# End of a cross-attention stage: row norms moved into the last step, norm rows transposed first, exponentials between value copies, gate products behind

## The reference

```python
# first attention: 16 heads of width 128, 64 context rows per batch entry
q = (hidden_states @ Wq).reshape(B, Sq, H, D)
k = (encoder_hidden_states @ Wk).reshape(B, Skv, H, D)
v = (encoder_hidden_states @ Wv).reshape(B, Skv, H, D)
q = rmsnorm(q, gq)
k = rmsnorm(k, gk)
scores = jnp.einsum('bqhd,bkhd->bhqk', q, k) * scale
attn = jax.nn.softmax(scores, axis=-1)
out = jnp.einsum('bhqk,bkhd->bqhd', attn, v)
out = out.reshape(B, Sq, H * D)
return out @ Wo
...
# routing of the first mixture, on the layer norm of the updated x
logits = x.astype(jnp.float32) @ router_weight.astype(jnp.float32).T
scores = jax.nn.sigmoid(logits)
sc = scores + e_bias
...
# expert that all tokens share
return jax.nn.silu(x @ sh_gate) * (x @ sh_up) @ sh_down
...
x = x + jnp.tanh(g_xattn[0]) * _L0_xattn_ref(_layernorm(x, axis=-1), ctx_1024, ...)
x = x + jnp.tanh(g_ffn[0]) * _L0_ffn_ref(_layernorm(x, axis=-1), ...)
```

## Time and profile before

| | |
|---|---|
| median of 3 runs | 1200.52 us (1198.31 to 1205.0) |
| profiled execution | 1197.71 us, span 1196.0 us |
| PE busy | 940.9 us, 79% of the span |
| DVE busy | 717.1 us, 60% |
| ACT busy | 430.6 us, 36% |
| POOL busy | 277.6 us, 23% |
| granted TensorE clock, mean | 0.878 |

### The profile page before, as it was taken

The page is one execution under the profiler, slowest core; times in us unless marked ns, Lnnn a source line. Parts: engine busy times, 40 slices in busy tenths (PEclk is TensorE's granted clock), DMA queues, the critical chain, the costliest instruction groups (busy, mean ns, idle before and its releaser), DMA issues.

```text
span 1196.0 us, 16300 instructions
## 1 busy us (share of the span) xinstructions
PE 940.9 (79%) x5499; PEld 792.4 (66%) x5499; DVE 717.1 (60%) x1677; ACT 430.6 (36%) x809; POOL 277.6 (23%) x225
## 2 busy tenths in 40 slices
PE   4998999999977700766676746868868999999998
PEld 3877868868855500655565533544547989899898
DVE  7267677686479998222222577988976445444343
ACT  4556446565463400111111114444453233323322
POOL 0332304314200000678888710101100000000000
PEclk9998999999988655778878867998868999999899
DMA  8002200000000060688888563000000000000000
GB/s 297 4 1 71 83 1 1 1 1 1 1 1 22 22 167 0 153 176 180 182 170 174 96 189 146 1 3 1 1 1 1 1 19 1 1 18 0 18 1 18
DMA packets 58945, 66.48 MB, mean 56 GB/s; under 512 B 5069, under 2 KB 55687, under 8 KB 58119
## 3 DMA queue, kind: packets, MB, share of 16 engines
q1 hardware_dynamic: 45236, 46.45, 12.5%
q0 software_dynamic: 12288, 18.88, 8.9%
q10 hardware_dynamic: 1363, 0.37, 0.1%
HBM read 48.13 MB, written 17.56 MB: 55 GB/s over the span
## 4 chain that ended last, share of the span: by engine, by line
PE 53%; DVE 23%; issue 10%; POOL 5%; DMA 4%; ACT 4%; ACTq 0%; DVEq 0%; POOLq 0%; SPq 0%
PE bank L2062 13%; PE bank L1753 7%; PE bank L2088 7%; PE bank L1738 4%; PE bank L1710 3%; POOL acc L507 3%; DMA acc<-y,dst_now 3%; PE bank L1946 3%; PE bank L1729 2%; POOL xg L497 2%; PE bank L2073 2%; DVE cand L926 2%; DVE keyT L929 2%; DVE newton L582 1%; DVE small L1071 1%
## 5 line engine op out<-in xcount | busy, mean ns | idle before, releaser
L2062 PE MATMUL bank<-gu_hi,xnT_split 128*128 128x352 f32 x640 | 164.0, 330 | 4.9 <-DVE soft L1249 3.7
L486 POOL TENSOR_TENSOR q_lo<-soft,q_hi 128x512 fp32r<-128x512 f32 x64 | 91.3, 1426 | 226.0 <-ACT soft L1385 225.9
L2062 PEld LDWEIGHTS bank<-gu_hi,xnT_split 128*128 128x128 f32 x640 | 114.6, 192 | 5.6 <-DVE soft L1249 3.9
L507 POOL DMA_INDIRECT acc<-y,dst_now x64 | 102.5, 1602 | 26.3 <-issue 20.2
L2062 PE MATMUL bank<-gu_lo,xnT_split 128*128 128x352 f32 x320 | 104.4, 326 | 0.0
L732 DVE COPY qT<-bank 128x512 f32<-128x512 f32 x64 | 44.2, 691 | 91.7 <-PE bank L1753 91.1
L1249 DVE SCALAR_TENSOR_TENSOR soft<-sg,combine_w,bank 128x176 f32<-128x176 f32 x160 | 56.4, 395 | 70.9 <-PE bank L2062 65.3
L497 POOL DMA_INDIRECT xg<-table,src_now x64 | 64.1, 1002 | 116.6 <-DVE src_now L959 97.4
L979 DVE TENSOR_SCALAR y<-bank,xg 128x256 f32<-128x256 f32 x64 | 28.0, 479 | 95.9 <-PE bank L1874 80.2
L1598 ACT ACTIVATE sg<-bank 128x352 f32<-128x352 f32 x80 | 37.1, 465 | 127.3 <-PE bank L2062 123.3
L1861 PEld LDWEIGHTS bank<-xgT,w_gu 128*88 128x88 f32 x512 | 76.8, 196 | 7.3 <-issue 5.1
(11 more groups left out here) (271 smaller groups left out, 2209.4 us busy)
## 6 DMA issues: line engine op xcount, KB each, us to landing
w_gu<-in_L_ffn_w_gu SPq DMA_DIRECT2D x32, 352.0 KB
w_dn<-in_L_ffn_w_down SPq DMA_DIRECT2D x32, 176.0 KB
acc<-zeros SPq DMA_DIRECT2D x2, 2176.0 KB
acc_rows<-acc SPq DMA_DIRECT2D x8, 512.0 KB, 4.9
gu<-in_L_gu SPq DMA_DIRECT2D x1, 3520.0 KB, 13.4
table<-xw SPq DMA_DIRECT2D x4, 640.0 KB, 3.5
wo<-in_L_xattn_Wo SPq DMA_DIRECT2D x2, 1024.0 KB, 15.6
wq<-in_L_xattn_Wq SPq DMA_DIRECT2D x1, 2048.0 KB, 17.9
```

The costliest lines, as they stand in the source:

```text
L486: pool.tensor_tensor(q2_lo[:, h % 3, :], q2[h % 2], q2_hi[:, h % 3, :], ALU.subtract).then_inc(q2_split, 1)
L507: pool.indirect_dma_start(acc[e], bass.IndirectOffsetOnAxis(ap=dst_now[:, q, e:e + 1], axis=0), y[:, q, e, :], None, compute_op=ALU.add).t ...
L2062: mm = pe.matmul(b[:, 0:2 * F1], v[:, c, j * P:(j + 1) * P], w[:, c, p, o, :], start=(n == 0), stop=(n == len(terms) - 1))
```

## The change

VectorE: the last step now makes the row statistics and roots of group 0 behind heads 12 and 15 and applies them before it copies `n_rows`; the residual of tile 3 of group 2 goes behind Newton's steps; `normed(0)` behind the step is gone; `shared_product(0)` moves from the softmax loop into `route(0)`, behind the keys. ScalarE: the tokens and the table rows are copied first; the eight value banks are copied in three portions, one behind each of the exponentials 0, 1 and 2; then come the sigmoid, `attn_out(0)`, exponential 3, and the other `attn_out`; the silu moves behind the end of the stage. TensorE: `n_rows` is transposed before the output of tile 3 of group 2; then token transposes, that output, the logits, the values, the tiles of group 3; the gate products move behind the end of the stage.

```diff
@@ VectorE
-                    if h == 12 and not last:
-                        row_stats(i + 1)
-                    if h == 15 and not last:
+                    if h == 12:
+                        row_stats(0 if last else i + 1)
+                    if h == 15:
                         row_roots(EPS0)
-                if not last:
-                    row_apply(i + 1)
+                row_apply(0 if last else i + 1)
...
-                if not first_:
+                if not (first_ or last):
                     out(3)
...
                 inverse_root(rq[:], qvar[:], G * H0)
+                if last:
+                    out(3)
...
-            normed(0, EPS0)
             first_group = 0
...
-                if j == 2:
-                    shared_product(0)
...
+                if i is first_group:
+                    shared_product(i)
@@ ScalarE
-                values_in(0, 8 if last else 4)
-                if not last:
+                if not last:
+                    values_in(0, 4)
                     keys_in()
...
             first_group = 0
-            exponential(NG - 1, 0, (NG - 1) % 2)
             tr.at(T2 - T_HEADS)
-            route_front(first_group)
-            for j in range(G):
-                if j + 1 < G:
-                    exponential(NG - 1, j + 1, (NG - 1) % 2)
+            rows_in(first_group)
+            for j in range(3):
+                exponential(NG - 1, j, (NG - 1) % 2)
+                values_in(3 * j, min(3 * j + 3, 8))
+            sigmoids(first_group)
+            attn_out(0)
+            exponential(NG - 1, G - 1, (NG - 1) % 2)
+            for j in range(1, G):
                 attn_out(j)
             act.drain().then_inc(done1["act"], 1)
             for e in done1.values():
                 act.wait_ge(e, 1)
+            silus(first_group)
@@ TensorE
-                if not first_:
-                    output(i - 1, G - 1, 0 if last else C)
+                if not (first_ or last):
+                    output(i - 1, G - 1, C)
...
-                values(i % 2, 0, 8 if last else 4)
-                if not last:
+                if not last:
+                    values(i % 2, 0, 4)
                     transpose_keys(i + 1)
...
             tr.at(T2 - T_HEADS)
-            route_front(0)
+            transpose_xn(NG, False)
+            output(NG - 2, G - 1, C)
+            tr.evacuated(pe)
+            logits_out()
+            values((NG - 1) % 2, 0, 8)
             for j in range(G):
                 transpose_attn(NG - 1, j)
                 output(NG - 1, j)
             pe.drain().then_inc(done1["pe"], 1)
+            shared_gates(0)
```

More of the change, by code:

```diff
@@ L1406, in _, with rows_in @@
             step(NG - 1, False, True)
-            def route_front(i):
-                sr.at(S2, SR, i)
+            def rows_in(i):
                 for c in range(C):
@@ L1414, in route_front, with sigmoids, silus @@
                 act.activation(xw[:, i % 2, :, 0:DIM], xn[:], ACT.Copy)
+            def sigmoids(i):
                 act.activation(sigs[:, i % 2, :], tr.read(act)[:, 0:G * E0], ACT.Sigmoid).then_inc(t_ring.free, 1)
+            def silus(i):
+                sr.at(S2, SR, i)
                 if i is not first_group:
@@ L1420, in route_front @@
                                    ACT.Silu).then_inc(s_ring.free, 1)
+            def route_front(i):
+                rows_in(i)
+                sigmoids(i)
+                silus(i)
             first_group = 0
-            exponential(NG - 1, 0, (NG - 1) % 2)
             tr.at(T2 - T_HEADS)
-            route_front(first_group)
-            for j in range(G):
-                if j + 1 < G:
-                    exponential(NG - 1, j + 1, (NG - 1) % 2)
+            rows_in(first_group)
[6 more added lines that the diff above has]
+            for j in range(1, G):
                 attn_out(j)
@@ L1786, in _, with logits_out @@
             step(NG - 1, False, True)
[L1787 to L1790, removed]
+            def logits_out():
                 b = tr.fill(pe)
@@ L1796, in route_front, with shared_gates @@
                 mm.then_inc(t_ring.full, 1)
+            def shared_gates(i):
+                qr.at(Q2, QR, i)
+                sr.at(S2, SR, i)
                 for half in range(2):
@@ L1804, in route_front @@
                         mm.then_inc(ring.full, 1)
+            def route_front(i):
+                transpose_xn(NG + i)
+                logits_out()
+                shared_gates(i)
             pe.wait_ge(r_loaded, 64)
             tr.at(T2 - T_HEADS)
-            route_front(0)
+            transpose_xn(NG, False)
+            output(NG - 2, G - 1, C)
+            tr.evacuated(pe)
+            logits_out()
+            values((NG - 1) % 2, 0, 8)
             for j in range(G):
```

## The result

Timed beside the kernel before on the same chip, the changed kernel takes 1209.27 us (median of 7 runs, 1207.67 to 1211.42) against 1201.08 (7 runs, 1198.31 to 1205.0). The ratio of the runs is **1.0066, 95% interval 1.0053 to 1.0080**: 7.9 us slower. The profiled execution took 1209.81 us, 1208.1 of them span (before: 1197.71 and 1196.0), at a mean granted clock of 0.872.

What follows compares the result with a forecast made beforehand. VectorE was taken to lead, held up now and then. O0 + O1 - 7.55 gave +4.4 us: 1202.1 on the profiled run, 1204.9 on the median's scale, stated as 1204.5; range 1197.5 to 1211.

Steps and rivals of the forecast that it cites:

- the rival with three outputs at the low clock: Tile 3's output also falls to 6.77 us, with the first two outputs slow: +9.1 us, 1209.6; chance 0.23.
- O0 and O1: Times of the output products of tiles 0 and 1, last softmax group: taken as 5.2 and 6.77 us, bounds 3.72 to 6.77.
- my sum: Whole change: O0 + O1 - 7.55 us, the last divide's shift plus 1.3 at the routing; +4.4 forecast.
- Part 1: Row norms of routing group 0 moved inside the last step: VectorE gains 5.66 us, for a few tenths.
- Part 2: Norm rows transposed before group 2's tile 3 output: first by_norm at 327.5, 6.9 us earlier than 334.39.
- Part 3: Softmax loop, exponentials placed between value copies: tile 1's sums lose their 2.92 us wait.
- The new wait before `divide(1)`: VectorE in the softmax loop: logits hold a transpose bank until the sigmoid, some 4 us (sign: 3 to 5).
- The wait before residual 1: VectorE in the softmax loop: exponential 3, behind residual 0, delays output 1; idle 3 to 7 us.
- The tail: Routing, residual 2 to the next norms: 12.66 instead of 11.37 us, cost 1.3; 4.3 with a slow last output.
- The sign I wrote for it: Sign of being right, in the routing: group 1's norms waiting for the sigmoid; no size given.
- The rule weighed: Skill's drain of about 1380 ns beside ScalarE's sigmoid table load: sum 1.4 us higher; the row without drain was kept.
- Full gain: Logits bank doesn't hold back the transposes; softmax ends 12.3 us earlier, less 1.3: 1189.5; chance 0.10.

Runs made afterwards that it cites:

- norms_only: The kernel before, with only the row norms of group 0 made in the last step; timed ratio 0.9971.
- sig_early: The changed kernel with the sigmoid of routing group 0 ahead of the exponentials on ScalarE; timed ratio 1.0056 to the kernel before.
- out1_first: The changed kernel with ScalarE's copies of tile 1's transposes ahead of exponential 3; timed ratio 1.0014 to the kernel before.
- all3: The changed kernel with the moves of sig_early, out1_first and gates_in_gap together; timed ratio 0.9988 to the kernel before.
- filler: The changed kernel with five extra unused TensorE products behind the transposes of tile 1; timed ratio 1.0059 to the kernel before.
- gates_in_gap: The changed kernel with group 0's gate products before the last output and silu before the stage end; ratio 1.0055 to the kernel before.
- norms_gap: The kernel before with group 0's row norms in the last step, gates before the last output, shared_product(0) in routing; 1194.74 us, ratio 0.9952.

## Why the prediction was right or wrong

The range, 1197.5 to 1211, holds the measured time, near its top; the forecast of 1204.5 is 4.8 us short. What came about is the rival with three outputs at the low clock, which I gave 0.23. Slower by over 0.5% had 0.29 against 0.62 for no change. That this rival's 1209.6 meets the measured 1209.27 so closely is luck: it has 6.77 us for each of O0 and O1, 1.8 more in sum than they took, and lacks the 3.1 us by which `divide(1)` came late. With the measured O0 and O1 and the measured tail my sum would give 11.76 - 7.55 + 2.5 = +6.7, for +9.8 in place and +7.9 timed. By steps:

- **Part 1, 5.66 us of norms moved**: right in itself. norms_only shows the first `by_norm` 5.8 us earlier in place. That the gain then doesn't reach the end is also as forecast, but norms_only kept more of it, 3.1 us, than the 1.5 I expected of that run: the logits behind the shorter gap of 2.75 us ran 2.00 us, not the 3.27 of rows 4, and the gate products behind them 5.33, not 5.74.
- **Part 2, norm rows first**: wrong in sign. I had the first `by_norm` at 10.7 us after head 15's copy; it came at 331.74 - 318.48 = 13.26. Two terms were missing. The output of tile 3 of group 2 now stands behind a short wait and the four small transposes and ran at 0.50: 5.16 instead of 3.72, 1.44 us, directly in front of the residual. This isn't the scatter of one execution: it takes 4.75 to 5.16 us in all seven kernels with the norm rows first and 3.67 in the other five. And the roots, from 319.09 to 323.85, took 4.76 instead of 3.68 (below), 1.08 us. norms_only, which has the roots at the same place but not Part 2, is at 11.83: Part 2 costs 1.4 us here instead of bringing 1.2. It wasn't run alone.
- **Part 3, exponentials between copies**: the wait of 2.92 us went, as forecast.
- **The new wait before `divide(1)`**: forecast some 4 us (3 to 5 as the sign of being right) and named with its cause; measured 5.21, and sig_early removes it. It came 33.93 us after head 15's copy instead of 30.7: Part 2's delay passed through, and the half of the transposes behind the sigmoid took 1.12 us where I had counted 0.6.
- **The wait before residual 1**: forecast 3 to 7 us, measured 5.81, with the chain as written; out1_first removes it.
- **O0 and O1**: 5.43 and 6.33 for 5.2 and 6.77, in sum 11.76 for 11.97. With 11.76 the sum for the last divide gives +2.9; the 3.1 more that were measured are the late `divide(1)`. This, with Part 2 behind it, is the first and larger mis-sized term.
- **The tail**: +3.8 for 1.3. The chain I wrote (last output, gates, sigmoid) is there, but I had the output at 3.69 and it took 6.42. The idle time before it, 4.32, was forecast as 3.6 and set aside as a rival. Having taken the low clock behind two gaps of 4 and 5 us, I had no row that spoke for the full clock behind a third of 3.6, only the row of before where the gap is 0.87. This is the second error, 2.5 us: the rival should have been the forecast. The sign I wrote for it says "group 1's norms"; those that wait for the sigmoid of group 1 are the norms of group 2, as the sum has it.
- **The rule weighed**: in the changed kernel the last copy ends at 349.06 + 0.37 = 349.43, the load runs from 349.45 to 350.73, the sigmoid starts at 350.74. No extra time stands before or behind the load, and keeping the row was right.
- **Full gain**, 1189.5: refuted by the 5.21 us, and even without any of the three costs (all3) the new order gives 0.9988.

What isn't settled: why O0 and O2 run at the full clock in some of these kernels and not in others (below), whether they do so in every execution of the same kernel, and how much of all3's missing gain is the clock and how much ScalarE's queue.

## What to carry to other kernels

Removing a wait of one engine is worth only what the next queue lets through: before moving an operation ahead in a queue, write down what stands behind it and which shared bank or buffer it keeps open, as here a logits bank and `attn_out(1)`. Count each new gap on TensorE twice, once for itself and once as up to 3 us on the dependent product behind it, and move independent products into the gap that stands in front of a product on the path. Time each part of a combined reordering alone: here Part 1 alone gained 3.5 us, and the whole lost 7.9.

## What the runs showed of the hardware

- **A long idle time of TensorE and a low clock go together, but the last gap alone doesn't tell the clock.** For the last output it does, in all twelve kernels: behind 4.32 us idle it took 5.97 to 6.51 us, behind 2.43 us 5.38, and behind 1.02 us or less 3.62 to 3.69. So does it for output 1: 6.32 to 6.52 behind 5.52, 3.72 behind 1.23 or less. Filling the gap brought the full clock in both places (filler, gates_in_gap). For output 0 it doesn't: 3.72 behind 2.07 and even 3.19 (sig_early), 6.73 behind 2.21 (norms_gap). There the clock had fallen before the gap, while the transposes of tile 0 ran, behind an earlier gap of 2.75 us and the logits. Windows view of norms_gap, columns as in rows 1:

```profile
341.00:343.00 2.00, 1.61 (x8) 1.09 (x6) 1.85 (x2) 1.96 (x4) 0.00 (x0) 0.50 0.00 0
```

  In the changed kernel too it was at 0.50 in 350 to 352 already, before output 0 at 352.99. Every one of the twelve profiles has at least one of the four products at the low clock, for part of its time or all of it.
- **A tiny operation of VectorE can take as long as GpSimd's beside it.** Timeline of the changed kernel, both engines:

```profile
320.43 1.28 POOL L486 TENSOR_TENSOR q_lo<-soft,q_hi 128x512 fp32r<-128x512 f32 x1 [1.38 <-ACT soft L1385]
320.47 1.25 DVE L582 SCALAR_TENSOR_TENSOR newton<-newton,var 128x4 f32<-128x4 f32 x1
...
322.15 0.16 DVE L582 SCALAR_TENSOR_TENSOR newton<-newton,var 128x4 f32<-128x4 f32 x1
```

  The same line takes 0.16 us when GpSimd is idle, and 1.25 when it starts 0.04 behind a GpSimd operation of 1.28. The Trainium skill, "SBUF — State Buffer", section Who interferes with whom, says that an operation of VectorE with two inputs in SBUF contends with one of GpSimd that reads SBUF, and that the order of issue decides which of the two is blocked; the trace agrees, with 0.16 us alone and 1.25 behind the GpSimd operation. The moved norms now run beside such an operation, where before (328.73 on) GpSimd was idle; this is the 1.08 us above.
